# Projections in four column tiles of 32, and an order of TensorE's steps of its own for each cycle, in three cross-attentions

## The reference

```python
q = query @ wq_w.T + wq_b      # query = layernorm(x): 4 x 512 x 256
k = value @ wk_w.T + wk_b      # value = ctx_1024:     4 x 1601 x 256
v = value @ wv_w.T + wv_b
scores = einsum('bhqd,bhkd->bhqk', q, k) / sqrt(16)
attn = softmax(scores)         # in the second cross-attention: sigmoid
ctx = einsum('bhqk,bhkd->bhqd', attn, v)
x = x + ctx @ dense_w.T + dense_b
```

## Time and profile before

| | us |
|---|---|
| median of 3 runs (lowest, highest) | 2866.27 (2860.51, 2874.97) |
| profiled execution, first to last instruction | 2847.9 |
| PE (TensorE matmul) busy | 2704.7 |
| DVE (VectorE) busy | 1634.5 |
| ACT (ScalarE) busy | 1577.6 |

### The profile page before, as it was taken

How to read it: one execution, slowest core, us unless ns; L and a number is a source line. 1 busy time by engine, 2 the same in 40 slices (tenths; PEclk the granted TensorE clock), 3 DMA queues, 4 the chain that set the end, 5 groups by cost and what they waited for, 6 DMA issues and landing times.

```text
span 2847.9 us, 38377 instructions
## 1 busy us (share of the span) xinstructions
PE 2704.7 (95%) x14432; PEld 1338.9 (47%) x14432; DVE 1634.5 (57%) x3003; ACT 1577.6 (55%) x2687; POOL 289.1 (10%) x246
## 2 busy tenths in 40 slices
PE   7999999999899989999999999989989999999987
PEld 3334434343475647777333333358743343444433
DVE  6777778778375554442211221146677777877754
ACT  1677777777601112110677878842237777777764
POOL 2010100100011001111010110012211001010001
PEclk7899999999899999999999999999969999999998
DMA  5423334322200001001744445310043342333400
GB/s 115 70 35 36 59 42 64 42 29 24 90 1 30 0 15 52 1 1 35 116 49 70 57 67 62 68 49 1 12 58 53 41 70 31 41 58 37 47 1 30
DMA packets 68605, 125.13 MB, mean 44 GB/s; under 512 B 20980, under 2 KB 45119, under 8 KB 64967
## 3 DMA queue, kind: packets, MB, share of 16 engines
q1 hardware_dynamic: 67270, 120.25, 27.5%
q10 hardware_dynamic: 1152, 2.44, 0.4%
HBM read 42.11 MB, written 2.10 MB: 16 GB/s over the span
## 4 chain that ended last, share of the span: by engine, by line
PE 82%; DVE 9%; ACT 4%; issue 2%; SPq 2%; DMA 0%; ACTq 0%; POOL 0%; POOLq 0%; DVEq 0%
PE psum L190 53%; PE psum L733 20%; PE psum L1985 6%; DVE mpart L923 5%; ACT probs L801 3%; SPq L1039 1%; PE psum L286 1%; PE psum L743 1%; PE psum L1978 1%; SPq L1040 0%; DVE stats L313 0%; PE psum L752 0%; DVE hrow L338 0%; DVE parts L1806 0%; SPq L617 0%
## 5 line engine op out<-in xcount | busy, mean ns | idle before, releaser
L801 ACT ACTIVATE probs<-psum 128x512 f32<-128x512 f32 (+3 forms) x2080 | 1280.0, 692 | 387.6 <-PE psum L190 385.8
L923 DVE TENSOR_REDUCE mpart<-psum 128x2 f32<-128x804 f32 x1024 | 976.6, 991 | 309.8 <-PE psum L190 300.9
L733 PE MATMUL psum<-probs,vt 128*17 128x512 f32 (+1 forms) x4992 | 672.1, 614 | 1.4 <-ACT probs L801 1.4
L190 PE MATMUL psum<-qst,kst 50*128 50x512 f32 (+3 forms) x2496 | 610.2, 454 | 16.2 <-ACT probs L801 5.1
L190 PEld LDWEIGHTS psum<-qst,kst 50*128 50x128 f32 (+3 forms) x2496 | 270.8, 186 | 421.6 <-issue 268.4
L190 PE MATMUL psum<-kst,qst 48*128 48x402 f32 x2048 | 414.9, 429 | 41.0 <-DVE mpart L923 38.7
L190 PEld LDWEIGHTS psum<-kst,qst 48*128 48x128 f32 x2048 | 199.3, 197 | 349.9 <-issue 183.9
L190 PE MATMUL psum<-wv,ctxT 128*128 128x256 f32 (+1 forms) x624 | 184.0, 422 | 1.1 <-DVE vt L913 0.5
L733 PEld LDWEIGHTS psum<-probs,vt 128*17 128x17 f32 (+1 forms) x4992 | 85.2, 96 | 201.8 <-issue 160.8
L190 PE MATMUL psum<-ctxT,wk 128*128 128x512 f32 (+1 forms) x384 | 158.2, 542 | 10.8 <-DMA ctxT<-in_ctxT 9.3
L190 PEld LDWEIGHTS psum<-wv,ctxT 128*128 128x128 f32 (+1 forms) x624 | 109.6, 195 | 78.1 <-issue 59.7
(11 more groups left out here) (323 smaller groups left out, 2683.2 us busy)
## 6 DMA issues: line engine op xcount, KB each, us to landing
kst<-kp_hi SPq DMA_DIRECT2D x144, 200.1 KB, 5.8
ctxT<-in_ctxT SPq DMA_DIRECT2D x36, 512.0 KB, 5.5
kst<-kp_lo SPq DMA_DIRECT2D x72, 200.1 KB, 5.4
qst<-qp_hi SPq DMA_DIRECT2D x144, 64.0 KB, 4.5
kst<-kp_hi SPq DMA_DIRECT2D x84, 100.1 KB, 2.9
qst<-qp_lo SPq DMA_DIRECT2D x72, 64.0 KB, 5.1
kst<-kp_lo SPq DMA_DIRECT2D x42, 100.1 KB, 3.0
stage<-in_L_ffn_W SPq DMA_DIRECT2D x16, 256.0 KB, 4.0
```

The source lines that it names most:

```text
L190: last = e.matmul(dst, lhsT, rhs, start=i == 0, stop=i == len(pairs) - 1)
L733: t = e.matmul(c.bank(self.acc)[32 * h:32 * h + VW, :], self.vt[0:kn, kc, self.head(g, h), :], p[0:kn, h % self.wide, :], start=kc == 0, s ...
L801: e.activation(self.probs[n % slots][0:kn, :, :], c.psum[0:kn, k:k + self.wide, :], ACT.Exp if softmax else ACT.Sigmoid, scale=DH ** -0.5) ...
L923: e.tensor_reduce(self.mpart[:, :, p * (SEQ // P) + qt, i], c.psum[:, k:k + 2, 0:MAX_WIDTH], AX.X, ALU.max).then_inc(c.drained(k), 1)
```

## The change

- A new helper `mm4` writes each product of 128 stationary columns as four products of 32, each in its own column tile (form B). `keys`, `query`, `values` and `proj` use it instead of `mm`. The arithmetic and the operands are the same; a value projection has 8 matmul instructions in place of 2.
- `CYCLE` and `LAST_CYCLE` are replaced by `ORDERS`, which has a string of letters for each softmax flag, each group `g` and each cycle `i`. The letter `f` takes the next step of the slot; what a string leaves over is put at the end of the cycle.

```diff
-CYCLE = "wssvxssv", "sswmmssvssmxmssvmm"
-LAST_CYCLE = "wssvvx", "wssvmsxsmv"
+ORDERS = (
...
+        ("ssfvfssv", "sfvsssvf", "ssvvss", "sfvsssv", "fssvvss", "sfvsssv", "fssvv"),
...
+        ("smmssmsssmsmmsvv", "msmssmssvmsssmvm", "msssmvmsssmvssmffm", "mssmsvmsssmvmssmff", "smmssvmssfmmsmssv", "fssmfmssvssmmsvmsm", "ssvmmssfv"),
...
+def mm4(e, dst, pairs):
+
+    for i, (lhsT, rhs) in enumerate(pairs):
+        for at in range(0, lhsT.shape[1], 32):
+            end = min(at + 32, lhsT.shape[1])
+            last = e.matmul(dst[at:end, :], lhsT[:, at:end], rhs, start=i == 0, stop=i == len(pairs) - 1,
+                            tile_position=(0, at))
     return last
...
-        maxima, slot = iter(self.cycle_maxima(u, i)), self.slot_steps(u, i)
...
+        taken = {"s": iter([("scores", f, u, kc, h) for kc in range(2 * i, min(2 * i + 2, len(KEY_CHUNKS)))
+                            for h in range(0, GROUP, self.wide)]),
+                 "m": iter(self.cycle_maxima(u, i)),
+                 "v": iter([("pv", f, u, kc) for kc in (2 * i - 2, 2 * i - 1)] if i else [("pv", f, u - 1, LAST_KC)] if u else []),
+                 "f": iter(self.slot_steps(u, i))}
+        steps = [step for letter in ORDERS[self.softmax][u % GROUPS][i] for step in [next(taken[letter], None)] if step]
+        steps += [step for letter in "smvf" for step in taken[letter]]
...
-                mm(e, bank[0:kn, 0:DM], [(self.ctxT[:, q, k0:k0 + kn], self.wv[:, q, :])
+                mm4(e, bank[0:kn, 0:DM], [(self.ctxT[:, q, k0:k0 + kn], self.wv[:, q, :])
```

More of the change, by code:

```diff
@@ L49 @@
 PROBS = 16
[L52 to L53 removed]
+ORDERS = (
+    (
+        ("sssvfvs", "sfvsssv", "fssvvss", "svfssvs", "sfvsssv", "fsssvfvs", "ssvv"),
+        ("ssfvfssv", "sfvsssvf", "ssvvss", "sfvsssv", "fssvvss", "sfvsssv", "fssvv"),
+        ("fsssvfsv", "sfvsfssv", "fsssvvs", "sfsssvfv", "sfssvvs", "svssvs", "svsv"),
+        ("ssvvss", "vssvss", "fssvvss", "sfvfsssv", "fssvvss", "svfssvfs", "ssfvv"),
+    ),
+    (
+        ("msssmvmvsssmmssmf", "msmssvssmsmvssmmf", "msmssvmsssmvssmffm", "msmssvmsssmvssmmff", "smsmsvsssvmssmffmm", "ssvmssmvssmfmssfmm", "svmsssmv"),
+        ("mssfsmsmsfmsmsmsvv", "fmssmsvmsssmvmsmsf", "msmssvmsssmvssmmf", "smsmssfvmssmsvmsm", "ssmvssmsmvssmfmsm", "svsmsmsvsmssmfmsm", "svmmssfvs"),
+        ("smfmssvsmsfsmsvmms", "fsfsmmvsmssmssmsmv", "msssmvmsssmvssmffm", "mmssvmssfmmsmsvfss", "msmsvssmsmvssmsfm", "vmmsssvsmsssmsmm", "svmssmvs"),
+        ("smmssmsssmsmmsvv", "msmssmssvmsssmvm", "msssmvmsssmvssmffm", "mssmsvmsssmvmssmff", "smmssvmssfmmsmssv", "fssmfmssvssmmsvmsm", "ssvmmssfv"),
+    ),
+)
 VW = DH + 1
@@ L192, in mm @@
             last = e.matmul(dst, lhsT, rhs, start=i == 0, stop=i == len(pairs) - 1, tile_position=tile_position)
+    return last
+def mm4(e, dst, pairs):
[4 more added lines that the diff above has]
+                            tile_position=(0, at))
     return last
@@ L665, in tensor @@
                     e.wait_ge(c.sem(f"ctx_in{n}"), 16 * (BATCH * self.past + b + 1))
-                mm(e, bank[:, 0:kn], [(self.wk[:, q, cc * P:(cc + 1) * P], self.ctxT[:, q, k0:k0 + kn])
+                mm4(e, bank[:, 0:kn], [(self.wk[:, q, cc * P:(cc + 1) * P], self.ctxT[:, q, k0:k0 + kn])
                                       for q in range(KC)]).then_inc(c.filled(k), 1)
@@ L673, in tensor @@
                     e.wait_ge(*norm.hT_made(f, b))
-                mm(e, bank, [(self.wq[:, q, cc * P:(cc + 1) * P], c.hT[:, q, rows_of(b)])
+                mm4(e, bank, [(self.wq[:, q, cc * P:(cc + 1) * P], c.hT[:, q, rows_of(b)])
                              for q in range(KC)]).then_inc(c.filled(k), 1)
@@ L762, in tensor @@
                 left = self.cT if softmax else self.ctxn[b % 2]
-                mm(e, bank[:, 0:DM], [(left[:, g, t * P:(t + 1) * P], self.wo[:, g, :])
+                mm4(e, bank[:, 0:DM], [(left[:, g, t * P:(t + 1) * P], self.wo[:, g, :])
                                       for g in range(left.shape[1])]).then_inc(c.filled(k), 1)
```

## The result

| us | before | after |
|---|---|---|
| median of 5 runs (lowest, highest) | 2862.36 (2853.66, 2874.97) | 2787.33 (2765.47, 2791.24) |
| profiled execution, span | 2847.9 | 2763.7 |
| first softmax attention, first to last `pv` | 670.4 | 633.6 |
| sigmoid attention | 484.5 | 458.7 |
| second softmax attention | 684.3 | 664.5 |

After takes 0.9723 of the time before (95% interval 0.9684 to 0.9763): 75 us less by the medians, 84 by the two spans. The forecast was 2765 us and 101 less. The profiled execution of after is the fastest of its five; it took 2765.47 us, so only 1.8 us lie around a span, not the 18.4 that the prediction took. The rest of that 18.4 was the distance of one fast execution from the median of its kernel.

What follows compares the result with a forecast made beforehand. PE, busy 95% of the span, was taken as the bound, by its steps and the gaps between them. Softmax 76 plus sigmoid 25 is 101 us off 2847.9, giving 2747; with 18.4 above the span, 2765 us, range 2705 to 2845.

Steps and rivals of the forecast that it cites:

- Term 1: All three attentions: fewer and cheaper changes of PE's tile form; 17 us less in each softmax attention, 29 in sigmoid.
- Term 2: Projections as four column tiles: as many column passes on PE; costed at nothing, 5 us either way.
- Term 3: Softmax attentions: the new order removes PE's waits; 58 us each at most, 38 taken, 76 for both, 0 to 116.
- the walks: Softmax cycles stepped through: with projection 5.7 us, 0.4 less; without, 4.8 us, 1.0 less; two thirds taken.
- waits stay: Rival, 2841 us, chance 0.17: only sigmoid's 25 us come; in softmax, split pairs cost the 17 us the forms give.
- Sigmoid: Sigmoid attention: fewer form changes gain as far as PE is last; 25 of 29 us taken, range 10 to 30.
- Issue binds: Rival, 2981 us, chance 0.08: PE can't beat 57 ns per record; a value step takes 1.84 instead of 0.86 us.
- A sequencer's pace: Rival, 2796 us, chance 0.10: rounds of 256 columns take 0.248 instead of 0.213 us; 31 us go back.

Runs made afterwards that it cites:

- e1_forms: The kernel before with `mm4` alone, in the old order of steps; 2837.5 us, 0.9883 of before.
- e5_after_again: The repetition: the changed kernel as it is, run once more; 2782.0 us, 0.9725 of before.

## Why the prediction was right

**The sign, the size and the range** held: 2787 us lies in 2705 to 2845, 22 above the forecast. Of these 22, 16.8 are the span (2763.7 in place of 2746.9), and 5.2 the place of the profiled execution among its fellows: 23.6 us under the median after, where 18.4 was taken.

**What a change of form costs, Term 1.** Right in its prices. Entering B with 32 columns was taken as 0.02 to 0.03 and measures 0.03; leaving 0.11, here 1.00 (a value step between two maxima in `e1_forms`) less 0.86 and 0.03. The rows of `e1_forms`:

```profile
402.44 0.34 PE L190 MATMUL psum<-kst,qst 48*128 48x402 f32 x2
402.71 1.07 PE L201 MATMUL psum<-wv,ctxT 128*32 128x256 f32 x16
403.71 0.45 PE L190 MATMUL psum<-kst,qst 48*128 48x402 f32 x2
```

The counts were a little high: between the first and the last `pv` the traces have 642 changes before and 587 after in the first softmax attention (forecast 660 and 605), 489 and 341 in the sigmoid one (493 and 345). At the prediction's prices that is 16 and 29 us less, for 17 and 29 forecast. But only part of it shows as time. The forms alone gained 7 and 6 us at full clock in softmax, and all changes in the sigmoid attention 20.

**Term 2, columns.** Four column tiles cost next to no columns: 0.216 us a round against 0.213.

**Term 3, waits in softmax.** In the batches in the middle it held: the walks give 5 x 1.0 + 19 x 0.4 = 12.6 us for one with five cycles without projection, two thirds of it are 8.4, and 8.8 and 9.2 came in the first attention. Over the whole the two attentions gave 36.8 and 19.8 us for 38 each. The clock accounts for the difference between the two: after's second attention had 0.89 in its first 98 us and 0.91 in the next 100, its first attention 0.99 over all; in before both had 0.97. By the clock's record 18 and 22 us were lost to it before, and 8 and 33 after. Without them the gains are 27 and 31 us, 58 together for 76.

The **step that failed** is the 1.0 us that Term 3 puts on each of the 33 cycles without projection. It was read from one cycle of 5.79 us with two maxima close together. In the four cycles shown above, at full clock, 0.4 to 0.5 came of it. And 12 of the 33 stand in the last two units of the last batch, where nothing was gained; the walk's share for them was 8 us in each attention. These two units, in the first attention, before and after:

```profile
683.43:752.00 68.57, 62.33 (x380) 21.03 (x379) 27.79 (x49) 54.26 (x107) 1.02 (x1) 0.88 0.10 32
```

```profile
645.68:712.50 66.82, 61.30 (x381) 21.31 (x380) 27.81 (x49) 54.90 (x108) 1.02 (x1) 0.92 0.11 33
```

At full clock that is 60 us before and 62 after, and in the second attention 75 and 74; the repetition has 60 and 75. The two units ahead of them gained 4.1 and 4.0 us at a clock of 1.00, the walk's two thirds being 4.8. The prediction could have seen a part of it: maxima are made for the unit that comes next, so the last unit and the last full cycle of the one before it have none, 7 of the 12 cycles, and no wait for a maximum to save. Why the other five gained nothing stays open. In the second attention PE idles in these units and its clock falls:

```profile
2665.00:2670.00 5.00, 3.98 (x11) 1.43 (x9) 0.00 (x0) 2.30 (x6) 0.00 (x0) 0.80 0.00 2
2670.00:2675.00 5.00, 3.30 (x6) 1.34 (x6) 0.00 (x0) 2.26 (x4) 0.00 (x0) 0.50 0.00 0
```

There they took 87.3 us in place of 82.1. Whether these idle times come from the strings of the last units was not tried.

**Why** the waits fell was argued too narrowly. The prediction saw two maxima close together and a DVE that comes late. The trace names it so, and reducing half of the columns on DVE (136 to 85 us in a batch) gained 1.2 us of 175. Taking a third off ACT's work (131 to 90 us) gained 5.5. In this trace a wait that two engines hold together shows the name of the last one only.

**The walk of one cycle** in isolation is the larger gap. It said 5.7 us for `msssmvmsssmvssmffm` and never laid this string behind itself; put in every cycle (with one string in the sigmoid attention too), it is slower than before by 0.8%, and by 9 and 8 us at full clock in the softmax attentions. So the walk was no ground for the forecast; the table, which has another string at most seams, came out near it, and the prediction had not walked the table. That part is luck. The sentence "a step early in one place is late in another" under the rival *waits stay* was the true danger, and it deserved its 0.17.

**Sigmoid.** 25.8 for 25, 458.7 us for 460. Some 5 us of it are clock (0.98 before, 0.99 after); at full clock 20 came for 25.

**The rivals.** *Issue binds* fell: a value step takes 0.89 us, not 1.84. *A sequencer's pace* fell too: 0.216 us a round, not 0.248, in each of the value steps shown. The rule of the Trainium skill, "TensorE: Matmul & The Clock Gate", section "Wait — 56ns, not 53.3ns?", 62 ns for a MATMUL, would have had 0.248; the rounds here do not agree with it. The page says it of a chip without hardware decode, and no run shows which way this one decodes. DVE's share, forecast at 78% or more, is 77% in the attention at 0.99.

## What to carry to other kernels

When a product is cut into column tiles of the same form as its neighbours, it costs next to no columns (0.216 us a round for 0.213) and saves both changes, some 0.2 us a time here. Where other engines hold PE up, as in softmax here, the order of the steps was worth four times as much. An order for engines that share small rings of banks is worth what its seams are worth: write out two cycles in a row with the step that evacuates each bank, and with the slots that really occur, before trusting a pattern. And read a wait's name as the last of several: cut each candidate's work in turn before believing it. Last, count the cycles to which a saving applies; here a part of them had nothing to save.

## What was not expected of the hardware

The granted clock of one core fell while PE was busy without a gap. In `e5_after_again`, in the same code and place where after stayed at full clock (second fence):

```profile
364.00:367.00 3.00, 3.00 (x18) 1.62 (x17) 2.88 (x4) 2.67 (x6) 0.00 (x0) 1.00 0.62 68
367.00:370.00 3.00, 3.00 (x16) 0.98 (x17) 2.35 (x3) 2.35 (x6) 0.00 (x0) 0.78 0.88 90
370.00:375.00 5.00, 5.00 (x23) 2.66 (x23) 2.80 (x3) 3.82 (x7) 0.00 (x0) 0.50 0.97 116
```

```profile
364.00:401.00 37.00, 36.73 (x330) 15.26 (x328) 28.65 (x35) 28.74 (x58) 0.00 (x0) 1.00 0.39 44
```

It stayed at 1.2 GHz (0.50) for about 20 us, and the unit took 45.8 us in place of 37.2. This episode cost 8.6 us. The DMA share of 0.97 beside it is not the difference: after had 1.07 and 1.08 in the same two stretches, from 367 to 375 us, at a clock of 1.00 (a packet counts where it starts, so a share can pass 1). The spread of one kernel goes the same way: the five executions of after took 2765, 2781, 2787, 2790 and 2791 us at mean clocks of 0.954, 0.946, 0.945, 0.943 and 0.942. What sets them off, no run shows. Whoever compares single executions of this kernel at less than 1% compares such episodes, which is why batches at clock 1.00 and lengths at full clock were used above.
